# Quarter transfers, a wider first composition stage and a new instruction order in a gated-aggregation and triple-convolution kernel

## The chip, the cores and the metric

The kernel runs on one core of a Trainium2 chip. The metric is device microseconds of one execution. Engines are named as the profile names them: PE is TensorE (PEld its weight loads), DVE is VectorE, ACT is ScalarE, POOL is GpSimd, SP is SyncE, which here issues every DMA.

## The reference, cut to what matters

The input x is 8 images of 32 channels by 64 x 64, float32. `_gn` with 32 groups over 32 channels is a normalisation of each channel of each image.

```python
def _forward(x, gate_w, gate_b, value_w, geom_w, geom_b, pw_w, pw_b):
    gate = einsum('bchw,rc->brhw', x, gate_w) + gate_b
    mu = softmax(gate, axis=1)
    v = einsum('bchw,dc->bdhw', x, value_w)
    patches = the 3x3 neighbours of v, zero padded
    g = einsum('bchw,gc->bghw', x, geom_w) + geom_b
    theta, raw_base, raw_hyp = g.reshape(Bb, 3, R, L)
    sig_u, sig_s = base * exp(hyper), base * exp(-hyper)
    kern = exp(-(pu / sig_u) ** 2 - (ps / sig_s) ** 2)
    w = mu * kern
    w = w / (sum(w, axis=(1, 2)) + 1e-06)
    agg = einsum('brsl,bcsl->brcl', w, patches)
    return einsum('bkhw,ok->bohw', agg, pw_w) + pw_b

x = x + _forward(_gn(x), ...)
x = x + conv3x3(conv3x3(conv3x3(_gn(x), w1), w2), w3)
```

Per pixel and each of R = 4 mixtures, nine tap weights are made from the pixel's own channels. The three convolutions in a row have nothing between them.

## The kernel before, in words

An image lies on 128 partitions as four quarters of 16 rows by 32 channels. Since the kernel of the taps is the same for opposite neighbours, nine taps become five: the pixel itself and four sums of opposite pairs.

For image i the steps are these. `load_x(i)` brings x into one of three buffers (`xraw`). `gn1_stats`, `gn1_sums` (two PE products that add up the quarters), `gn1_spread`, `gn1_scale`, `gn1_rstd` (POOL) and `gn1_bias` make the first norm's scale and shift. ACT applies them twice: `norm1` into `xc`, `norm1_padded` into `xn`, whose edge rows the two DMAs of `halo` fill; `pair_sum` (POOL) makes the pair sums `xs`. `geometry` is 8 PE products (16 records) into `geo_ps`. `tap_weights` is a chain of 29 small DVE operations with 7 ACT parts between them. `values` transposes one of ten units (five taps, two halves of the image) into one of two banks, and `mult` on DVE multiplies it with its tap weights, 2048 columns at a time (L1060). Each half needs four sums of products: per image and half the table `SUMS` says whether DVE (V, L1070), POOL (G, L1877) or PE (T, inside `transpose_sums`) makes each; images 1 to 7 have one G in each half, fourteen in all. `sums_out` (ACT) evicts, `pointwise` (PE) and `residual` (DVE) end the first block. `gn2_...` is the second norm (L887 is the third operation of `spread` in both norms, sixteen times in all), `norm2` writes `y`, and `by_slots` copies it by 16 DMAs of 32 partitions into `xq`, the layout in which the convolutions read it.

The three convolutions are composed into one of 7 x 7, with corrections for the edges. `turn` and `take_turn` turn the weights round; `first_weights` (PE, L380) composes w2 with w3 into `v_sb`, evicted by `take_first` (ACT); `second_weights` (PE, L403) composes that with w1, evicted by `take_second` (ACT) into `kb` and `kt`. Per image `convs` then makes 60 terms: for each half of the columns 14 main ones of 512 columns (L433), and small ones for rows, columns and corners at the edges. `conv_term` splits each into two products of 64 output channels that run side by side. `result` (ACT) evicts and `store` writes the image out.

Float32 products appear as two records each, transposes as one. Every engine's program is a straight list written out by hand (in the order that a search found), and engines wait for each other by semaphores; each engine, and SP's queue, runs its list strictly in order. So an instruction that waits holds everything behind it on its engine.

The change touches `load_x` (L254, with the weights' and constants' DMAs at L258 to L264 inside it, after image 0's load), `store` (L291), `first_weights` (L380), `take_first` (L1625), the waits that count their semaphores, and the five lists. In the list of before, PE began so:

```python
            fold(0, 0)
            turn(0)
            fold(0, 1)
            turn(1)
            gn1_sums(0, 0)
            first_weights(0)
            gn1_sums(0, 1)
            first_weights(1)
            geometry(0)
            first_weights(2)
            gn1_sums(1, 0)
            first_weights(3)
```

Of the kernel before, what the change touches and what calls it, by code (L numbers as in the profile page):

```python
# [12 lines left out]
G = 4  # L13
QR = H // G
# [38 lines left out]


PAIRS = (((0, 2),), ((0, 0),), ((0, 1), (1, 0)), ((0, 2), (1, 1), (2, 0)), ((1, 2), (2, 1)), ((2, 2),), ((2, 0),))
FIRST_SEGS = {0: ((0, 3, 1), (2, 1, 6)), 1: ((0, 3, 2),), 2: ((0, 3, 3), (0, 1, 0))}
# [19 lines left out]
def conv_l0_l1_kernel(nc, x, geo_w, geo_bias, val_w, pw_t, pw_b, w1, w2, w3, ident, sel_quarter,  # L76
                      masks, consts, out):
    ctx = ExitStack()
    with ctx:
# [6 lines left out]
        def sem(name):  # L86
# [50 lines left out]
            "p (e f) -> p e f", e=STEPS)  # L137
        outb = sb("outb", [P, 2, H // 4, W])
# [106 lines left out]
        def _(sp):  # L245
# [4 lines left out]
            def load_x(j):  # L250
                if j >= N_X:
                    wait(x2_done, 2 * (j - N_X) + 2)
                src = x[j, :, :, :].rearrange("c (g r) w -> g c (r w)", g=G)
                sp.dma_start(xraw[:, j % N_X, :], src).then_inc(x_in[j % N_X], 16)  # L254
                if j == 0:
                    for dst, src in ((sel1_sb, sel_quarter), (val_w_sb, val_w), (geo_w_sb, geo_w),
                                     (geo_bias_sb, geo_bias)):
                        sp.dma_start(dst[:, :], src).then_inc(front_consts_in, 16)  # L258
                    for dst, src in ((consts_sb, consts), (ident_sb, ident), (pw_t_sb, pw_t), (pw_b_sb, pw_b)):
# [49 lines left out]
            by_slots(1, 3)  # L309
            store(0)  # L310
            halo(4)
# [12 lines left out]
            store(2)  # L324
            load_x(7)
            halo(6)
# [22 lines left out]
            for n in range(2):  # L349
                wait(out_st[n], 16 * (IMAGES // 2))  # L350

        @block.tensor
        def _(pe):
# [16 lines left out]
            def first_weights(n):  # L370

                if n == 0:
                    pe.wait_ge(turned, 2)
                if n >= N_CONV:
                    pe.wait_ge(v_out, n + 1 - N_CONV)
                rows = range(2 * n, min(2 * n + 2, STEPS))
                terms = [(e, a, b, seg) for e in rows for a in PAIRS[e] for b in range(3) for seg in FIRST_SEGS[b]]
                for k, (e, (a, a2), b2, (b, m, at)) in enumerate(terms):
                    to = (e - 2 * n) * STEPS * C + at * C
                    mm = nc.tensor.matmul(conv_ps[n % N_CONV][:, to:to + m * C], w2_sb[:, 2 * b2 + a2 if a2 < 2 else 6 + b2, :],  # L380
                                          w3_sb[:, b:b + m, 2 - a, :], start=k == 0,
                                          stop=k == len(terms) - 1, skip_group_check=True)
                mm.then_inc(first_pe, 1)

            def second_weights(n, part):

                if n == 0 and part == 0:
                    pe.wait_ge(v_out, 4)
# [3 lines left out]
                for seg in range(max(len(SEGS[b]) for b in range(3)) * 3):  # L392
                    for half, i in enumerate(ROWS2[n]):
                        if part >= len(FROM[i]) or seg % 3 >= len(SEGS[seg // 3]):
# [9 lines left out]
                                              v_sb[rows, e, at * C:(at + m) * C], start=part == seg == 0, stop=last,  # L404
# [150 lines left out]

            fold(0, 0)
            turn(0)
            fold(0, 1)
            turn(1)
            gn1_sums(0, 0)  # L560
            first_weights(0)
            gn1_sums(0, 1)
            first_weights(1)
            geometry(0)
            first_weights(2)
            gn1_sums(1, 0)
            first_weights(3)
            values(0, 0)
            values(0, 1)
            second_weights(0, 0)  # L570
            gn1_sums(1, 1)
            second_weights(1, 0)
            second_weights(1, 1)
            geometry(1)
            second_weights(2, 0)
            second_weights(2, 1)
            gn1_sums(2, 0)
            second_weights(2, 2)
            values(0, 2)
            gn1_sums(2, 1)  # L580
            values(0, 3)
            second_weights(3, 0)
            second_weights(3, 1)
            second_weights(3, 2)
            values(0, 4)
            values(0, 5)
            second_weights(4, 0)
# [3 lines left out]
            values(0, 7)  # L591
            transpose_sums(0, 2)
            values(0, 8)
            transpose_sums(0, 3)
            values(0, 9)
            second_weights(4, 1)
            pointwise(0, 0)
            geometry(2)
            values(1, 0)
            second_weights(5, 0)  # L600
            values(1, 1)
# [3 lines left out]
            transpose_sums(0, 7)  # L605
            values(1, 2)
            second_weights(6, 0)
            pointwise(0, 1)
            values(1, 3)
            values(1, 4)  # L610
            values(1, 5)
            gn2_sums(0, 0)
            gn1_sums(3, 0)
            gn2_sums(0, 1)
            values(1, 6)
            transpose_sums(1, 0)
            transpose_sums(1, 1)
            values(1, 7)
# [1416 lines left out]
```

## Time and profile before

| what | us |
|---|---|
| three runs, in order | 532.97, 548.08, 546.44 |
| median | 546.44 |
| the profiled execution's own time | 540.62 |
| its span, first to last instruction | 538.7 |
| PE busy | 477.7 (89%) |
| DVE busy | 370.1 (69%) |
| ACT busy, POOL busy | 150.2, 145.2 |
| mean granted clock of TensorE | 0.94 |

The span is 1.9 us shorter than the execution's own time; what lies around it is start and end. Busy time is no measure of how well PE is used, only of when it has something to do. The idle time of an engine matters where the engine is the one that others wait for.

### The profile page before, as it was taken

Reading aid. Unit: us, or ns where it says so; the run is one execution under the profiler, and the core shown is the slowest. Engines: PE = TensorE matmul, PEld = TensorE weight load, DVE = VectorE, ACT = ScalarE, POOL = GpSimd, SP = SyncE. Lnnn points to the kernel's source line nnn. Section 1 sums busy time; section 2 is a strip of 40 time slices with the busy share of each in tenths; the row PEclk is TensorE's granted clock in tenths of the full one; section 3 lists DMA queues with packets and bytes.
Section 4 is the critical chain, followed back from the end, with each engine's and each line's share of the span. In section 5 each row is a group of like instructions: output and inputs, shape, how many; then the busy total and the mean of one; then the engine's idle time right before and its main releaser. Section 6 shows DMA issues by size and latency. Waiting matters only on the chain. (4 is left out here: it accounts for less than half of the span.)

```text
span 538.7 us, 8815 instructions
## 1 busy us (share of the span) xinstructions
PE 477.7 (89%) x3692; PEld 299.3 (56%) x3692; DVE 370.1 (69%) x499; ACT 150.2 (28%) x247; POOL 145.2 (27%) x75
## 2 busy tenths in 40 slices
PE   0898999954698979999999997999799999999991
PEld 0898899844454544564546453465357545554451
DVE  2213499996987996999599936998978669930000
ACT  0512726512340134121712072025211440111000
POOL 0150003331903370345035400382316103300000
PEclk9999669995999997999999998999969999999997
DMA  5200000000301031003112111201003103103201
GB/s 103 86 5 0 6 1 2 5 23 18 85 6 40 0 88 39 16 29 88 41 42 65 32 43 58 61 17 24 4 1 86 41 1 86 39 1 83 44 1 39
DMA packets 26967, 19.51 MB, mean 36 GB/s; under 512 B 21104, under 2 KB 21680, under 8 KB 26928
## 3 DMA queue, kind: packets, MB, share of 16 engines
q1 hardware_dynamic: 26928, 18.95, 14.6%
q8 instruction: 29, 0.48, 0.4%
q14 instruction: 10, 0.08, 0.0%
HBM read 5.16 MB, written 4.19 MB: 17 GB/s over the span
## 5 line engine op out<-in xcount | busy, mean ns | idle before, releaser
L433 PE MATMUL conv_ps<-xq,kb 128*64 128x512 f32 x768 | 190.1, 627 | 4.1 <-DMA xq<-y 2.4
L1060 DVE TENSOR_TENSOR prod<-val_ps,tapw 128x2048 f32<-128x2048 f32 x80 | 181.0, 2280 | 8.3 <-PE val_ps L486 7.3
L433 PEld LDWEIGHTS conv_ps<-xq,kb 128*64 128x64 f32 x768 | 56.5, 139 | 86.1 <-issue 85.7
L1877 POOL TENSOR_TENSOR prod<-prod 128x2048 f32<-128x2048 f32 x14 | 64.0, 4569 | 92.8 <-DVE prod L1060 92.8
L1903 POOL TENSOR_TENSOR xs<-xn 128x1024 f32<-128x1024 f32 x32 | 68.6, 2158 | 69.5 <-PE val_ps L486 66.9
L503 PEld LDWEIGHTS agg_ps<-ident_sb,prod 128*128 128x128 f32 x688 | 76.4, 143 | 15.9 <-issue 11.7
L503 PE MATMUL agg_ps<-ident_sb,prod 128*128 128x128 f32 x688 | 83.0, 276 | 0.8 <-DVE prod L1070 0.8
L1653 ACT ACTIVATE agg<-agg_ps 128x512 f32<-128x512 f32 x64 | 37.9, 596 | 90.7 <-PE agg_ps L503 90.4
L1070 DVE TENSOR_TENSOR prod<-prod 128x2048 f32<-128x2048 f32 x23 | 54.3, 2359 | 0.0
L486 PE MATMUL val_ps<-ident_sb,xs 128*128 128x128 f32 x256 | 43.8, 298 | 6.2 <-DVE prod L1060 6.2
L486 PEld LDWEIGHTS val_ps<-ident_sb,xs 128*128 128x128 f32 x256 | 30.5, 152 | 27.1 <-issue 13.5
L1670 ACT ACTIVATE outb<-conv_ps,gn 128x512 f32<-128x512 f32 x16 | 11.0, 686 | 97.3 <-PE conv_ps L447 97.3
L1863 POOL TENSOR_TENSOR gn<-gn 128x1 f32<-128x1 f32 x8 | 6.6, 823 | 102.7 <-DVE gn L892 102.7
L433 PE MATMUL conv_ps<-xq,wmid 128*64 128x512 f32 x128 | 32.2, 610 | 0.0
L403 PE MATMUL conv_ps<-xq,w_sb 64*128 64x160 f32 (+2 forms) x154 | 24.6, 374 | 1.9 <-ACT kb L1647 1.9
L1867 POOL TENSOR_TENSOR gn<-gn,powers 128x2 f32<-128x2 f32 x8 | 6.0, 747 | 75.0 <-DVE gn L892 75.0
L380 PE MATMUL conv_ps<-outb,w_sb 64*128 64x96 f32 (+1 forms) x110 | 24.3, 410 | 0.0
L380 PEld LDWEIGHTS conv_ps<-outb,w_sb 64*128 64x128 f32 x110 | 23.7, 328 | 0.2
L403 PE MATMUL conv_ps<-xq,w1n_sb 64*128 64x32 f32 (+2 forms) x168 | 22.9, 334 | 0.6 <-ACT kt L1647 0.6
L468 PEld LDWEIGHTS geo_ps<-geo_w_sb,xc 128*128 128x128 f32 x128 | 19.2, 238 | 6.4 <-issue 4.1
L436 PEld LDWEIGHTS conv_ps<-xq,kt 128*64 128x64 f32 x448 | 16.4, 137 | 10.6 <-issue 10.6
L403 PEld LDWEIGHTS conv_ps<-xq,w1n_sb 64*128 64x128 f32 x168 | 21.0, 256 | 1.4 <-ACT kt L1647 0.9
(116 smaller groups left out, 445.4 us busy)
## 6 DMA issues: line engine op xcount, KB each, us to landing
xq<-y SPq DMA_DIRECT2D x128, 70.0 KB, 2.1
xraw<-in_x SPq DMA_DIRECT2D x8, 512.0 KB
out_y<-outb SPq DMA_DIRECT2D x8, 512.0 KB
xn<-xn SPq DMA_DIRECT2D x16, 24.8 KB, 1.8
outb<-in_w SPq DMA_DIRECT2D x1, 384.0 KB, 5.6
outb<-in_w SPq DMA_DIRECT2D x1, 192.0 KB, 8.4
outb<-in_w SPq DMA_DIRECT2D x1, 96.0 KB, 5.7
sel_sb<-in_sel_quarter SPq DMA_DIRECT2D x1, 64.0 KB, 3.4
```

Of the source, the lines that this page charges most:

```text
L380: mm = nc.tensor.matmul(conv_ps[n % N_CONV][:, to:to + m * C], w2_sb[:, 2 * b2 + a2 if a2 < 2 else 6 + b2, :], w3_sb[:, b:b + m, 2 - a, :] ...
L403: mm = nc.tensor.matmul(conv_ps[half][:, to * C:(to + m) * C], w[rows, 4 * b + half + a, :], v_sb[rows, e, at * C:(at + m) * C], start=par ...
L433: mm = nc.tensor.matmul(bank[part, :], w, src[:, every, cols], start=n == 0, stop=False)
L436: mm = nc.tensor.matmul(bank[part, q * W // 2:(q + 1) * W // 2], kt[:, half, LEFT + m, :], src[:, line, cols], start=False, stop=False)
L468: mm = nc.tensor.matmul(geo_ps[:, k * GEO:(k + 1) * GEO], xc[:, i % 2, k * P:(k + 1) * P], geo_w_sb[:, :], start=k == 0, stop=k == K8 - 1, ...
L486: mm = nc.tensor.matmul(val_ps[u % 2][:, kk * P:(kk + 1) * P], src, ident_sb[:, :], is_transpose=True, start=kk == 0, stop=kk == KK - 1, s ...
L503: mm = nc.tensor.matmul(agg_ps[n % N_AGG][:, kk * P:(kk + 1) * P], product(i, TAPS * h + b)[:, at0:at0 + P], ident_sb[:, :], is_transpose= ...
L1060: v.tensor_tensor(dst, val.unsqueeze(2).to_broadcast([P, B, R, C]), wgt.unsqueeze(3).to_broadcast([P, B, R, C]), ALU.mult).then_inc(mult_d ...
L1070: v.tensor_tensor(product(i, TAPS * h + a), product(i, TAPS * h + a), product(i, TAPS * h + b), ALU.add).then_inc(add_v, 1)
L1653: s.activation(agg[:, n % G, :], agg_ps[n % N_AGG][:, :], ACT.Copy).then_inc(agg_sb, 1)
L1877: p.tensor_tensor(product(i, TAPS * h + a), product(i, TAPS * h + a), product(i, TAPS * h + b), ALU.add).then_inc(add_g, 1)
L1903: p.tensor_tensor(xs[:, n], xn[:, a[0], a[1]], xn[:, b[0], b[1]], ALU.add).then_inc(pairs_done, 1)
```

## The change

Every load of an image, and every store, becomes four DMAs of 32 partitions, and what waits for them counts 64 in place of 16. The constants and weights have a function of their own: eight constants go behind image 0's load, the three weight tensors behind image 1's. `first_weights` makes 34 products in place of 55, with more columns in each, in eight pieces (three parts each of pieces 0 and 1, one each of 2 and 3) that the list can place singly; pieces 0 and 1 make half of the 32 output channels each, for the inner 5 x 5 steps, 2 and 3 the edges and corners. The rows of `v_sb` lie the other way round, and `take_first` has five evictions in place of four. The lists of all five engines are in a new order; `SUMS` and the number of product buffers are as before, and no sum goes by DMA, as in the kernel before.

```diff
-                src = x[j, :, :, :].rearrange("c (g r) w -> g c (r w)", g=G)
-                sp.dma_start(xraw[:, j % N_X, :], src).then_inc(x_in[j % N_X], 16)
+                for g in range(G):
+                    sp.dma_start(xraw[C * g:C * g + C, j % N_X, :],
+                                 x[j, :, QR * g:QR * g + QR, :].rearrange("c r w -> c (r w)")).then_inc(x_in[j % N_X], 16)
+
+            def load_weights(n):
+                if n == 0:
+                    for dst, src in ((sel1_sb, sel_quarter), (geo_w_sb, geo_w), (geo_bias_sb, geo_bias),
+                                     (val_w_sb, val_w)):
                         sp.dma_start(dst[:, :], src).then_inc(front_consts_in, 16)
+                elif n == 1:
+                    for dst, src in ((ident_sb, ident), (consts_sb, consts), (pw_t_sb, pw_t), (pw_b_sb, pw_b)):
                         sp.dma_start(dst[:, :], src).then_inc(back_consts_in, 16)
+                else:
...
-                dst = out[j, :, :, :].rearrange("c (q s) w -> s c q w", s=4)
-                sp.dma_start(dst, outb[:, j % 2, :, :]).then_inc(out_st[j % 2], 16)
+                for s in range(4):
+                    dst = out[j, :, :, :].rearrange("c (q s) w -> c q s w", s=4)[:, :, s, :]
+                    sp.dma_start(dst, outb[C * s:C * s + C, j % 2, :, :]).then_inc(out_st[j % 2], 16)
 
             load_x(0)
+            load_weights(0)
+            load_weights(1)
             load_x(1)
+            load_weights(2)
             load_x(2)
...
+            def first_weights(n, part):
+
+                bank = conv_ps[n % N_CONV]
+                if part == 0:
+                    if n < N_CONV:
+                        pe.wait_ge(turned, 2)
+                    else:
+                        pe.wait_ge(v_out, n + 1 - N_CONV)
+                if n < 2:
+                    to = bank[:, 0:25 * C // 2].rearrange("p (e f o) -> p e f o", e=5, f=5)
+                    src = w3_sb[:, :, 0:3, n * C // 2:(n + 1) * C // 2].rearrange("p b r o -> p r b o")
+                    terms = [(part, b, to[:, 2 - part:5 - part, b:b + 3, :], src) for b in range(3)]
+                elif n == 2:
+                    edge = bank[:, 0:10 * C].rearrange("p (e f) -> p e f", e=2)
+                    corner = bank[:, 10 * C:14 * C].rearrange("p (e f o) -> p e f o", e=2, f=2)
+                    terms = [(0, b, edge[:, 0, b * C:(b + 3) * C], w3_sb[:, :, 0, :]) for b in range(3)]
+                    terms += [(2, b, edge[:, 1, b * C:(b + 3) * C], w3_sb[:, :, 2, :]) for b in range(3)]
+                    terms += [(2 * e, 2 - 2 * f, corner[:, e, f], w3_sb[:, 2 * f, 2 * e, :])
+                              for e in range(2) for f in range(2)]
+                else:
+                    edge = bank[:, 0:10 * C].rearrange("p (f e) -> p f e", f=2)
+                    terms = [(a, 2 - 2 * f, edge[:, f, (2 - a) * C:(5 - a) * C],
+                              w3_sb[:, 2 * f, 0:3, :].rearrange("p r o -> p (r o)")) for f in range(2) for a in range(3)]
+                end = n >= 2 or part == 2
+                for k, (a2, b2, to, src) in enumerate(terms):
+                    mm = nc.tensor.matmul(to, w2_sb[:, 2 * b2 + a2 if a2 < 2 else 6 + b2, :], src,
+                                          start=part == k == 0, stop=end and k == len(terms) - 1, skip_group_check=True)
+                if end:
+                    mm.then_inc(first_pe, 1)
...
+            gn1_sums(0, 0)
+            gn1_sums(0, 1)
             fold(0, 0)
+            fold(0, 1)
+            geometry(0)
             turn(0)
-            fold(0, 1)
             turn(1)
...
             gn1_sums(1, 0)
             values(0, 0)
             values(0, 1)
+            gn1_sums(1, 1)
+            first_weights(0, 0)
+            first_weights(0, 1)
+            first_weights(0, 2)
+            first_weights(1, 0)
+            first_weights(1, 1)
+            first_weights(1, 2)
+            first_weights(2, 0)
+            geometry(1)
+            first_weights(3, 0)
             second_weights(0, 0)
...
             fold(0, 0)
+            norm1(0)
+            norm1_padded(0)
+            fold(0, 1)
+            tap_weights(0, 0)
             take_turn(0)
+            tap_weights(0, 1)
             take_turn(1)
             take_first(0)
-            fold(0, 1)
-            norm1_padded(0)
-            norm1(0)
+            tap_weights(0, 2)
+            norm1(1)
             take_first(1)
+            norm1_padded(1)
+            tap_weights(0, 3)
+            tap_weights(0, 4)
             take_first(2)
             take_first(3)
+            tap_weights(0, 5)
+            tap_weights(0, 6)
             take_second(0, 0)
             take_second(0, 1)
```

The second list in this diff is ACT's. On DVE, `gn1_stats(0)` goes ahead of `centre_table(0)`, which waits for the constants, and from image 0 to image 7 the operations of neighbouring steps are interleaved otherwise. Ahead of `gn2_bias(0)` DVE has, from the first mult on, all ten mults of image 0 and five of image 1. `convs(0, 0, 1)`, the first convolution term, stands on PE behind `values(1, 9)`; before it stood behind `values(2, 1)`.

## Rows read from the trace of the kernel before

**Rows 1.** Busy time by stage (us: span, PE, PEld, DVE, ACT, POOL; clock; DMA).

```profile
48.60:112.00 63.40, 59.68 (x541) 56.35 (x540) 50.49 (x79) 33.09 (x58) 10.59 (x6) 0.84 0.01 3
112.00:145.70 33.70, 15.64 (x111) 12.28 (x111) 28.84 (x37) 8.80 (x15) 16.88 (x7) 0.80 0.20 50
145.70:465.00 319.30, 306.28 (x2370) 167.46 (x2371) 268.56 (x333) 90.64 (x148) 107.30 (x44) 0.96 0.16 40
465.00:528.40 63.40, 62.47 (x524) 31.13 (x523) 11.03 (x16) 6.39 (x9) 1.05 (x2) 1.00 0.13 29
```

**Rows 2.** What PE waited for (total us, times, longest), whole span.

```profile
PE pw_ps L459 <- DMA pw_b_sb<-in_pw_b: 14.3, 1, 14.3
PE geo_ps L530 <- DVE mv L880: 10.1, 2, 8.0
...
PE geo_ps L530 <- DVE geo L946: 3.8, 1, 3.8
PE pw_ps L545 <- DVE gn L887: 3.4, 1, 3.4
```

**Rows 3.** Timeline (start, us): SP's issues, and DVE's first reads of two loads.

```profile
115.52 0.60 SPq L254 DMA_DIRECT2D xraw<-in_x  x1
...
125.31 1.29 DVE L878 BATCH_NORM_STATS2 st<-xraw 128x6 f32<-128x512 f32 x2 [4.00 <-DMA xraw<-in_x]
...
133.86 10.05 SPq L285 DMA_DIRECT2D xq<-y  x16
...
320.17 0.59 SPq L254 DMA_DIRECT2D xraw<-in_x  x1
...
327.80 1.29 DVE L878 BATCH_NORM_STATS2 st<-xraw 128x6 f32<-128x512 f32 x2 [4.51 <-DMA xraw<-in_x]
```

**Rows 4.** DMA issues: KB each, median us from issue to landing.

```profile
xq<-y SPq DMA_DIRECT2D x128, 70.0 KB, 2.1
...
pw_t_sb<-in_pw_t SPq DMA_DIRECT2D x1, 16.0 KB, 2.8
pw_b_sb<-in_pw_b SPq DMA_DIRECT2D x1, 0.5 KB, 9.4
```

**Rows 5.** Busy time in three short stretches (columns as in rows 1).

```profile
14.00:24.00 10.00, 9.04 (x41) 8.09 (x41) 2.35 (x9) 4.88 (x7) 0.55 (x1) 1.00 0.26 99
...
332.00:340.00 8.00, 6.82 (x26) 2.60 (x26) 8.00 (x7) 1.99 (x4) 2.40 (x1) 0.79 0.39 92
388.00:400.00 12.00, 10.29 (x40) 6.47 (x42) 8.46 (x6) 0.00 (x0) 2.35 (x2) 0.57 0.00 1
```

**Rows 6.** Timeline of SP: the issue of the last store.

```profile
528.44 0.60 SPq L291 DMA_DIRECT2D out_y<-outb  x1
```

**Rows 7.** Timeline, from the head to the first convolution: PE, DVE, ACT.

```profile
18.12 4.47 PE L380 MATMUL conv_ps<-outb,w_sb 64*128 64x96 f32 x20
...
23.03 10.87 PE L380 MATMUL conv_ps<-outb,w_sb 64*128 64x96 f32 x50
33.83 3.67 PE L468 MATMUL geo_ps<-geo_w_sb,xc 128*128 128x64 f32 x16
...
67.32 2.28 DVE L1060 TENSOR_TENSOR prod<-val_ps,tapw 128x2048 f32<-128x2048 f32 x1
...
132.47 1.26 ACT L1663 ACTIVATE y<-x,gn 128x1024 f32<-128x1024 f32 x1 [1.99 <-DVE gn L896]
...
145.69 1.54 PE L433 MATMUL conv_ps<-xq,kb 128*64 128x512 f32 x6 [1.69 <-issue]
```

**Rows 8.** The page's group of the first composition stage (busy us, mean ns).

```profile
L380 PE MATMUL conv_ps<-outb,w_sb 64*128 64x96 f32 (+1 forms) x110 | 24.3, 410 | 0.0
```

**Rows 9.** Timeline of POOL and DVE at 385 us.

```profile
385.12 4.51 POOL L1877 TENSOR_TENSOR prod<-prod 128x2048 f32<-128x2048 f32 x1 [9.38 <-DVE prod L1060]
385.21 4.45 DVE L887 SCALAR_TENSOR_TENSOR gn<-gn,mv 128x1 f32<-128x1 f32 x1
```

**Rows 10.** Line 887 alone: duration ns, min/median/max.

```profile
L887 DVE SCALAR_TENSOR_TENSOR gn<-gn,mv x16: 219/219/4445, 18.5 to 483.8; 128x1 f32<-128x1 f32 x16
```

More of the change, by code:

```diff
@@ L349, in _ @@
             for n in range(2):
[L350 removed]
+                wait(out_st[n], 64 * (IMAGES // 2))
         @block.tensor
@@ L403, in second_weights @@
                         mm = nc.tensor.matmul(conv_ps[half][:, to * C:(to + m) * C], w[rows, 4 * b + half + a, :],
-                                              v_sb[rows, e, at * C:(at + m) * C], start=part == seg == 0, stop=last,
+                                              v_sb[rows, STEPS - 1 - e, at * C:(at + m) * C], start=part == seg == 0, stop=last,
                                               skip_group_check=True)
@@ L591, in _ @@
             values(0, 7)
+            second_weights(3, 0)
             transpose_sums(0, 2)
+            transpose_sums(0, 3)
             values(0, 8)
-            transpose_sums(0, 3)
+            geometry(2)
+            pointwise(0, 0)
             values(0, 9)
-            second_weights(4, 1)
-            pointwise(0, 0)
-            geometry(2)
             values(1, 0)
-            second_weights(5, 0)
-            values(1, 1)
+            second_weights(3, 1)
             transpose_sums(0, 4)
@@ L689, in _ @@
+            values(3, 9)
+            convs(1, 43, 46)
+            geometry(5)
+            convs(1, 46, 56)
+            values(4, 0)
             transpose_sums(3, 0)
+            convs(1, 56, 60)
+            convs(2, 0, 1)
+            values(4, 1)
             transpose_sums(3, 1)
-            values(3, 7)
+            convs(2, 1, 2)
             transpose_sums(3, 2)
             transpose_sums(3, 3)
-            values(3, 8)
-            convs(1, 36, 37)
-            gn1_sums(5, 0)
+            convs(2, 2, 3)
@@ L1115, in _ @@
             gn1_scale(0)
+            centre_table(0)
             gn1_bias(0)
@@ L1203, in _ @@
             tap_weights(2, 5)
+            tap_weights(2, 6)
+            tap_weights(2, 7)
+            tap_weights(2, 8)
             mult(1, 1)
-            tap_weights(2, 6)
+            tap_weights(2, 9)
             mult(1, 2)
@@ L1482, in _ @@
             tap_weights(7, 3)
+            tap_weights(7, 4)
+            tap_weights(7, 5)
+            residual(5, 1)
+            tap_weights(7, 6)
+            gn2_stats(5, 1)
+            tap_weights(7, 7)
+            tap_weights(7, 8)
+            tap_weights(7, 9)
+            gn2_spread(5)
+            tap_weights(7, 10)
+            tap_weights(7, 11)
+            mult(6, 1)
+            gn2_scale(5)
+            tap_weights(7, 12)
+            mult(6, 2)
+            gn2_bias(5)
+            mult(6, 3)
+            tap_weights(7, 13)
+            add_products(6, 0, 1)
+            mult(6, 4)
+            mult(6, 5)
             mult(6, 6)
@@ L1724, in _ @@
             sums_out(0, 7)
-            take_second(6, 0)
+            take_second(3, 0)
             tap_weights(2, 2)
+            take_second(3, 1)
+            take_second(4, 0)
+            take_second(4, 1)
             tap_weights(2, 3)
+            tap_weights(2, 4)
+            take_second(5, 0)
             norm2(0)
-            tap_weights(2, 4)
+            tap_weights(2, 5)
             sums_out(1, 0)
+            take_second(5, 1)
             sums_out(1, 1)
```

805 lines of the change are left out of this document (376 added, 429 removed).

## Prediction

> **What bounds the kernel now.** I read the stages first [rows 1], then what TensorE waited for [rows 2], then the loads and stores behind the longest waits [rows 3 to 6], then the head [rows 7, 8]. The profiled span is 538.7 us, and TensorE is busy for 306.3 of the 319.3 us between 145.7 and 465, and for 62.5 of the 63.4 after them: in these stages it is the bound. It loses time in three places. At the start it waits 14.3 us for constants [rows 2]. Between 112 and 145.7 it works only 15.6 of 33.7 us, because the first image's chain on VectorE is late [rows 1]. At the end nothing but the last store runs: it is issued at 528.44, and the span ends 10.3 us after that [rows 6]. VectorE is second: 268.6 of 319.3 us, so 50.7 us of slack there.
>
> The loads of x are slow. That of image 3 is issued at 115.52, and VectorE, idle for 4.0 us, first reads it at 125.31: 9.8 us. That of image 7 takes from 320.17 to 327.80, 7.6 us, with VectorE idle for 4.5 [rows 3]. While nothing but x is being loaded (14 to 24 us), the DMA share is 0.26 at 99 GB/s, as if four of sixteen engines moved everything [rows 5].
>
> **The change: loads and stores.** Each 512 KB transfer becomes four of 32 partitions. The nearest row for such pieces is that of the slot copies: 16 of 70 KB, each 32 partitions wide, are issued within 10.05 us, 0.63 each [rows 3], and the page's issue list gives 2.1 us from issue to landing [rows 4]. Four pieces then cost 4 x 0.63 = 2.5 us of issue and, as the last one lands, 2.1 to 2.8 us more (2.8 is pw_t's) [rows 4]: some 5 us against 7.6 to 9.8. Lower end: 4 us, when issue alone counts; upper end: as now. I take 5. It adds 48 issues on SP's queue, 30 us over the span; what stands behind a load or store in that queue comes three issues (1.9 us) later: the slot copies above all, for which the convolutions wait. I cost that at nothing, as SP waits between them (a load at 115.52, the next copies at 133.86 [rows 3]); without that cover it is 1.9 us each time.
>
> The Trainium skill, DMA: Bandwidth & Descriptors, section "Why a DMA increments its semaphore by 16 and not by 1", says that the engines are counted from the outermost dimension of both patterns: 4 here before, 16 after. By that rule the share of 0.26 is no accident, and the trace agrees.
> The same page, section "Bandwidth", speaks against the change: it wants transfers gathered to a megabyte, and its fit has about 2 us fixed for each. If those fell one after another, four pieces would take about 9 us, an estimate from that page, and nothing would be won. The slot copies in a row every 0.63 us, each 2.1 us long, speak against that; it is a rival below.
>
> *End.* 10.3 us after the last issue become 2.5 of issue and 2.8 of landing, about 5.3: -5 us (bounds -6 and 0).
>
> *Start.* Before, the last constant that PE waits for landed 9.4 us after its issue, when the one issued just ahead of it needed 2.8 [rows 4]: I read it as their share on the four engines that still carried x. After: x's pieces end their issue at 0.73 + 4 x 0.6 = 3.1, eight constants at 0.47 follow to 6.9, and with 2.8 for landing the first four are there at 7.8, all at 9.7 (upper end: 14.3 as now).
>
> **The change: the order of the head.** Before, the first norm's second sum stood behind twenty products of the first composition stage (4.47 us), and geometry(0) behind fifty more (10.87 us), so geometry(0) ran at 33.83 for 3.67 us and VectorE started at 37.5 [rows 7]. After, PE does both sums, the folds and geometry(0) before anything else. From the first constants, 7.8: the norm's steps took 6.5 us with 4.0 of it in the queue, so 2.9 with centre_table between, 10.7; ScalarE, after fold, has normed at 12.0 (1.25 us); geometry 3.7: VectorE starts at 15.8, not 37.5.
>
> From there to the first mult took 29.8 us (to 67.32 [rows 7]). Now ScalarE's queue has take_first(0) ahead of tap_weights(0, 2), and take_first(2), (3) ahead of tap_weights(0, 5). Whatever waits behind them waits for the first composition, so that is on the path. Its cost: 110 records (two to a product; 66 of 96 columns and 44 of 32, a mean of 70) took 24.3 us [rows 8], 0.22 each. The 34 products are 68 records of 144 (36), 96 (24) and 32 columns (8). Six records of 512 columns, two side by side, take 1.54 us [rows 7], 0.51 a pair, so 1 ns a column, which leaves 0.15 us fixed: 36 x 0.294 + 24 x 0.246 + 8 x 0.182 = 17.9, against 24.3: -6.4 us. If runs of 16 numbers read slower than long runs, the saving falls to nothing (upper end, 24); if the fixed part is shared, 14 (lower end). The head is priced by the head's own rows throughout, slower as they are than later ones.
>
> PE after 15.8: turns, sums and two values to 20.3, first_weights(0) and (1) to 30.7, (2) to 35.3, geometry(1) to 38.9, (3) to 41.8, its eviction to 42.3. Then ScalarE's Square 0.6, VectorE 2.3, Exp 0.6, VectorE 3.4 and tap_weights(1, 0) 0.7: the first mult begins at 50, not 67.3: -17.3 us.
>
> **From the first mult to the first convolution.** Before: 65.2 us to the second norm at 132.47, then 13.2 for the norm and the 16 slot copies, to 145.69 [rows 7, 3]. In the new order VectorE has 15 mults of 2.28, three sums of 2.3, and small operations for 22 us ahead of gn2_bias(0): 63 us, and with waits as before but the load's 4.0 us some 68. So 50 + 68 + 13 = 131, against 145.7: -14.7. PE allows it: of its 75.3 busy us between 48.6 and 145.7 [rows 1] 74 remain, from second_weights(0) at 42, so 116 without idle time. Ends: 117 (-28) and 145.7 (0).
>
> **The long stage.** PE's work does not change here: 306.3 + 62.5 us. What can go is 13.0 + 0.9 us of idle time and the half-speed stretches. Two waits, of 2.1 us (10.1 less 8.0) and 3.8, end with a norm's sum or geometry behind a late load [rows 2]; after the second the clock is 0.79 for 8 us [rows 5], which costs 6.82 x 0.21 = 1.4, and I count as much for the first. With loads in 5 us these go: -8.7. Over the whole stage the clock is 0.96 [rows 1]: 306.3 x 0.04 = 12.3 us lost at the lower of its two levels, 1.2 and 2.4 GHz, of which 2.8 are counted. The other 9.5, and the other waits, 8.0, hang on the order; 7.8 of these 17.5 are one event, a wait of 3.4 us behind a VectorE instruction and 10.29 x 0.43 = 4.4 at 0.57 of the clock after it [rows 2, 5]. A new order may meet all of the 17.5 us again (0) or none (-17.5). I take a quarter away, -4.3, since that event looks like a coincidence. Sum for the stage: -13.
>
> **Sum.** Against the profiled execution's own time: -14.7 -13 -5 = -33, 538.7 to 506, and with the 1.9 us around the span (540.62 in all) 508 us. That execution lies 1% under the median of the three runs, 546.44, and between their ends.
>
> **The rivals.**
> *The long stage packs completely.* Against: every stage of before shows some wait. For: VectorE's 50.7 us of slack. From 131: 368.8 busy less the 12.3 of half clock, 0.7 of eviction, 5.3 of store and 1.9 around the span: 495; with the convolution at 124, 488. Time: 492.
> *The head's lead is lost before the convolutions*, since take_second stands in ScalarE's queue among the tap weights and PE's second stage waits for it. For: between 48.6 and 112 PE idles 3.7 us in that very stage [rows 1]. Then convolution 0 begins at 145.7 again: 508 + 14.7 = 523.
> *The pieces are no faster than the whole*, so the transfers' fixed time falls in a row: back come 8.7, 5 and 4.6 at the start: 526. This is also the case in which that part of the change does not do what it says.
> *Slower.* GpSimd's sums of 4.5 us hold up VectorE. At 385.21 an instruction of 0.22 us took 4.45, just as long as GpSimd's sum of 385.12 ran, and PE stood 3.4 us behind it [rows 2, 9]. Each such meeting in a norm's chain cost 3.4 + 4.4 = 7.8 us. There are 14 such sums, 16 such instructions, all newly ordered. From four more meetings on the gain is used up; at five the time is 508 + 39 = 547, and at six 555. Against: the median of the sixteen is 0.219 us [rows 10], one alone is long.
> The Trainium skill, SBUF — State Buffer, section "Who interferes with whom", has that as an exclusive lock: a two-input VectorE instruction blocks for the whole of a GpSimd instruction that reads the same memory. The row agrees.
>
> **How the numbers follow.** Forecast 508: 0.52 (its own range 498 to 520). Packed, 492: 0.18. Lead lost, 523: 0.15. Pieces no faster, 526: 0.06. Slower, 555: 0.03. The rest, 0.06, is lead lost and pieces slow together, some 538. The range is 488 to 527: it leaves out the slow ends (some 0.1) and little below. Over 2% faster (about what can be told from no change) means under 530 beside 540.6: 0.52 + 0.18 + 0.15 + 0.06 less 0.02 for runs near the edge: 0.89; within 2%: 0.08; slower: 0.03.
>
> **What would show it.** Geometry(0) near 12, the first mult near 50, the first convolution near 131; no VectorE wait for x; the last store's pieces landed some 5 us after the first issue; 68 records in the first composition, some 18 us. Wrong would be: a DMA share still near 0.3 in loads, the convolution not before 140, or new waits over 15 us in the long stage.

## The result, and the profile after

Four executions of the changed kernel took 507.69, 507.4, 509.83 and 507.81 us: a median of 507.75 against 541.43 for four of the kernel before (532.97 to 548.08, so they spread much more). The ratio is 0.950, 95% interval 0.944 to 0.957; it leaves out 548.08 and 546.44, two executions of the kernel before in a slower state, while the medians differ by 6.2%. So the change makes the kernel faster by 5 to 6%. The profiled execution took 507.69 us, its span is 505.6.

Lines have moved: L455 is the main convolution (L433 before), L402 the first composition, L1091 the mult, L918 the operation of the spread that was L887, L1921 POOL's sums.

Busy time by stage of the kernel after (columns as in [rows 1]). The stages are cut where the same work is left: 124.7, near the end of values (2,1), answers to 145.7 (there values (2,1) ended at 144.0, and PE then stood idle); 437, near the end of the last values, to 465; 500.4, the end of the last eviction, to 528.4.

```profile
39.20:87.00 47.80, 43.32 (x419) 40.41 (x420) 45.87 (x70) 21.93 (x41) 9.07 (x5) 1.00 0.01 2
87.00:124.70 37.70, 28.60 (x218) 23.63 (x217) 34.89 (x44) 16.58 (x27) 18.74 (x8) 0.83 0.18 45
124.70:437.00 312.30, 304.96 (x2373) 164.82 (x2372) 269.68 (x327) 87.90 (x144) 108.31 (x42) 0.98 0.18 40
437.00:500.40 63.40, 61.48 (x520) 30.86 (x516) 10.31 (x14) 6.35 (x9) 0.70 (x1) 1.00 0.16 32
```

Set beside [rows 1] this says where the 33.1 us of span went: 21.0 before the cut at 124.7 (145.7 - 124.7), 7.0 in the long stage (319.3 - 312.3), nothing in the next (63.4 in both), 5.1 after the last eviction (10.3 - 5.2). The cuts are good to about 1 us.

The timeline of the kernel after, rows that answer to [rows 6, 7] (PE, DVE, ACT and SP's queue):

```profile
0.73 1.79 SPq L252 DMA_DIRECT2D xraw<-in_x  x4
...
5.12 1.29 DVE L909 BATCH_NORM_STATS2 st<-xraw 128x6 f32<-128x512 f32 x2 [0.32 <-DMA xraw<-in_x]
...
10.99 3.67 PE L490 MATMUL geo_ps<-geo_w_sb,xc 128*128 128x64 f32 x16 [1.17 <-ACT xc L1594]
...
19.20 13.11 PE L402 MATMUL conv_ps<-outb,w_sb 64*128 64x144 f32 x56
...
35.85 2.87 PE L402 MATMUL conv_ps<-outb,w_sb 64*128 64x96 f32 x12
...
39.74 0.69 DVE L1024 TENSOR_TENSOR expo<-trig,ch 128x512 f32<-128x512 f32 x1 [5.68 <-ACT trig L1648]
...
46.31 2.28 DVE L1091 TENSOR_TENSOR prod<-val_ps,tapw 128x2048 f32<-128x2048 f32 x1
48.51 0.22 DVE L980 TENSOR_SCALAR ch<-geo 128x128 f32<-128x128 f32 x1
...
103.85 1.26 ACT L1707 ACTIVATE y<-x,gn 128x1024 f32<-128x1024 f32 x1
...
114.74 3.53 DVE L1030 TENSOR_TENSOR expo<-expo,trig 128x256 f32<-128x256 f32 x1
...
118.39 1.36 PE L455 MATMUL conv_ps<-xq,kb 128*64 128x512 f32 x4 [1.93 <-issue]
...
128.19 6.80 PE L455 MATMUL conv_ps<-xq,kb 128*64 128x512 f32 x20
...
500.52 2.61 SPq L295 DMA_DIRECT2D out_y<-outb  x4
```

Geometry(0) runs at 10.99 in place of 33.83, the first mult at 46.31 in place of 67.32, the second norm at 103.85 in place of 132.47. The lead is 28.6 us at the norm but 21.0 at equal work: the first convolution term stands alone at 118.39, and PE comes to the rest only at 128.19, behind two values and geometry(3); for the buffers of the values it waits 1.9 and 1.1 us for VectorE's mults. These mults stand behind L1030, a two-tensor operation that takes 0.42 us at the median and took 3.53 at 114.74, beside a sum of POOL's that ran from 113.46 to 117.98.

The waits of the kernel after, and its DMA issue list (columns as in [rows 2] and [rows 4]):

```profile
PE geo_ps L552 <- DVE mv L911: 7.9, 2, 6.8
PE pw_ps L567 <- DVE gn L918: 7.0, 3, 3.3
...
DVE st L909 <- DMA xraw<-in_x: 1.8, 2, 1.5
```
```profile
xraw<-in_x SPq DMA_DIRECT2D x32, 128.0 KB, 2.8
out_y<-outb SPq DMA_DIRECT2D x32, 128.0 KB, 2.7
```

PE's 14.3 us for constants are gone; it now starts at 6.8, with the norm's first sum, as soon as VectorE's statistics are there. The waits for late loads are all but gone too. What has grown is the wait behind VectorE's norm operation, from 3.4 us to 7.0. Its two long cases, in the timeline and in the durations of that line alone:

```profile
191.46 4.50 POOL L1921 TENSOR_TENSOR prod<-prod 128x2048 f32<-128x2048 f32 x1 [19.85 <-DVE prod L1091]
191.54 4.43 DVE L918 SCALAR_TENSOR_TENSOR gn<-gn,mv 128x1 f32<-128x1 f32 x1
...
196.03 0.38 PE L567 MATMUL pw_ps<-gn,sel_sb 128*128 128x1 f32 x2 [3.16 <-DVE gn L918]
...
407.82 4.43 DVE L918 SCALAR_TENSOR_TENSOR gn<-gn,mv 128x1 f32<-128x1 f32 x1
...
412.30 0.38 PE L567 MATMUL pw_ps<-gn,sel_sb 128*128 128x1 f32 x2 [3.28 <-DVE gn L918]
```
```profile
L918 DVE SCALAR_TENSOR_TENSOR gn<-gn,mv x16: 219/219/4433, 7.7 to 455.0; 128x1 f32<-128x1 f32 x16
```

This is the event of [rows 9, 10], met once before and twice now in the long stage. The two PE waits, 6.4 us, are nearly all of the 7.3 us that PE idles in the long stage.

### The profile page after: what moved, and what is told of

The parts are those of the page before. It is cut to its first block, busy times and chain, and to the rows that moved or that the text cites. A ratio compares the mean times of both kernels' runs of the same rounds, so it can differ in the third digit from the quotient of the medians.

```text
span 505.6 us, 8780 instructions
## 1 busy us (share of the span) xinstructions
PE 468.1 (93%) x3650; PEld 287.6 (57%) x3650; DVE 377.2 (75%) x499; ACT 150.6 (30%) x248; POOL 147.1 (29%) x75
## 3 DMA queue, kind: packets, MB, share of 16 engines
q1 hardware_dynamic: 27888, 18.95, 16.8%
## 4 chain that ended last, share of the span: by engine, by line
PE 66%; DVE 20%; issue 7%; SPq 2%; ACT 1%; POOL 1%; DMA 1%; POOLq 0%; DVEq 0%
PE conv_ps L455 34%; PE agg_ps L525 11%; DVE prod L1091 9%; PE val_ps L508 6%; PE geo_ps L490 4%; PE conv_ps L402 3%; DVE gn L918 2%; PE conv_ps L458 2%; SPq L288 2%; DVE prod L1101 2%; PE pw_ps L540 2%; PE conv_ps L465 2%; POOL prod L1921 1%; DVE expo L1030 1%; PE conv_ps L469 1%
## 5 line engine op out<-in xcount | busy, mean ns | idle before, releaser
L1091 DVE TENSOR_TENSOR prod<-val_ps,tapw 128x2048 f32<-128x2048 f32 x80 | 181.5, 2284 | 24.0 <-PE val_ps L508 18.9
L455 PE MATMUL conv_ps<-xq,kb 128*64 128x512 f32 x768 | 188.9, 623 | 3.2 <-issue 1.9
L455 PEld LDWEIGHTS conv_ps<-xq,kb 128*64 128x64 f32 x768 | 54.8, 139 | 87.8 <-issue 87.4
L1947 POOL TENSOR_TENSOR xs<-xn 128x1024 f32<-128x1024 f32 x32 | 71.1, 2231 | 97.1 <-PE val_ps L508 92.3
L1921 POOL TENSOR_TENSOR prod<-prod 128x2048 f32<-128x2048 f32 x14 | 63.8, 4560 | 121.0 <-DVE prod L1091 121.0
L525 PE MATMUL agg_ps<-ident_sb,prod 128*128 128x128 f32 x688 | 85.4, 279 | 2.9 <-DVE prod L1091 2.6
L455 PE MATMUL conv_ps<-xq,wmid 128*64 128x512 f32 x128 | 32.3, 611 | 0.0
L425 PE MATMUL conv_ps<-xq,w_sb 64*128 64x160 f32 (+2 forms) x154 | 22.6, 344 | 2.7 <-ACT kb L1691 2.2
L490 PE MATMUL geo_ps<-geo_w_sb,xc 128*128 128x64 f32 x128 | 20.8, 331 | 1.5 <-ACT xc L1594 1.5
L425 PE MATMUL conv_ps<-xq,w1n_sb 64*128 64x32 f32 (+2 forms) x168 | 21.2, 312 | 0.7 <-ACT kt L1691 0.7
L1109 DVE SCALAR_TENSOR_TENSOR x<-pw_ps,pw_b_sb,xraw 128x512 f32<-128x512 f32 x16 | 11.9, 745 | 11.7 <-PE pw_ps L540 11.7
L1707 ACT ACTIVATE y<-x,gn 128x1024 f32<-128x1024 f32 x8 | 10.1, 1257 | 31.9 <-DVE gn L927 31.9
L425 PEld LDWEIGHTS conv_ps<-xq,w1n_sb 64*128 64x128 f32 x168 | 18.7, 229 | 1.2 <-ACT kt L1691 1.0
```

What stands on the lines that cost most here:

```text
L425: mm = nc.tensor.matmul(conv_ps[half][:, to * C:(to + m) * C], w[rows, 4 * b + half + a, :], v_sb[rows, STEPS - 1 - e, at * C:(at + m) * C ...
L455: mm = nc.tensor.matmul(bank[part, :], w, src[:, every, cols], start=n == 0, stop=False)
L490: mm = nc.tensor.matmul(geo_ps[:, k * GEO:(k + 1) * GEO], xc[:, i % 2, k * P:(k + 1) * P], geo_w_sb[:, :], start=k == 0, stop=k == K8 - 1, ...
L525: mm = nc.tensor.matmul(agg_ps[n % N_AGG][:, kk * P:(kk + 1) * P], product(i, TAPS * h + b)[:, at0:at0 + P], ident_sb[:, :], is_transpose= ...
L1091: v.tensor_tensor(dst, val.unsqueeze(2).to_broadcast([P, B, R, C]), wgt.unsqueeze(3).to_broadcast([P, B, R, C]), ALU.mult).then_inc(mult_d ...
L1921: p.tensor_tensor(product(i, TAPS * h + a), product(i, TAPS * h + a), product(i, TAPS * h + b), ALU.add).then_inc(add_g, 1)
```

## The experiments

Theory: each part of the change pays about what the prediction gave it (loads 8.7 in the stage and 4.6 at the start, stores 5, the 34 products 6.4), and the new order would have paid more but for the two meetings with POOL. The main rival: the order alone carries the gain. Each time is the median of four executions or more (of three for a_first55). The kernel before, measured beside them, gave medians of 543.35, 541.5, 538.47 and 541.6 us, so a difference of under 5 us between kernels that were not measured side by side can't be read. The kernel after was not measured again beside the runs below.

**One part undone: loads whole (a_load1).**

```diff
-                for g in range(G):
-                    sp.dma_start(xraw[C * g:C * g + C, j % N_X, :],
...
+                src = x[j, :, :, :].rearrange("c (g r) w -> g c (r w)", g=G)
+                sp.dma_start(xraw[:, j % N_X, :], src).then_inc(x_in[j % N_X], 16)
```

> The kernel after, with each load of x as one transfer again (four pieces undone), all else as after (507.7 us). My theory, that a whole load is carried by four of sixteen engines: image 0's x lands near 11 us, not 5, the constants behind it near 14, geometry(0) begins near 16, not 10.99, and the loads of images 3, 6 and 7, first read 4 to 6.5 us after their issue now, are waited for by 2 to 4 us each: 514 to 523 us. Rival, pieces no faster than the whole, the order alone made room: 507 to 509 us, and VectorE's waits for x as after (1.8 us in all).

Measured: 520.97 us (519.99 to 522.51), +13.2. Waits and timeline of this kernel:

```profile
DVE st L908 <- DMA xraw<-in_x: 20.5, 7, 7.6
...
PE geo_ps L551 <- DVE mv L910: 17.3, 3, 14.1
```
```profile
12.40 1.29 DVE L908 BATCH_NORM_STATS2 st<-xraw 128x6 f32<-128x512 f32 x2 [7.61 <-DMA xraw<-in_x]
```

VectorE reads image 0 at 12.40; in the kernel after it did so at 5.12. That is 7.3 of the 13.2 us at the head; most of the rest lies in the long stage, with six later waits for x. The pieces pay.

**One part undone: stores whole (a_store1).** The four DMAs of `store` become the one of before.

> The kernel after, with each store as one transfer again. Theory: only the last store is on the path; its 5.1 us after the first issue become 10.3: 513 us. Rival, that the seven stores before it also hold up loads and slot copies on the shared queue: 516 or more, with waits of VectorE or PE for x or xq. Rival, nothing gained: 508.

Measured: 512.15 us (505.61 to 516.34), +4.4, with a span of 510.1 whose last store is issued at 499.87: 10.2 us to the end, as in [rows 6]. The spread is wide; the profile says the same.

**One part undone: the first stage in 55 products (a_first55).** `first_weights` and `take_first` of before, in the new order; parts 1 and 2 do nothing.

> The kernel after with the first composition stage of before (55 products in four blocks, placed where the pieces' first parts stand). Theory: take_first stands ahead of the tap weights in ScalarE's queue, so the 8 us more of this stage (24.3 against 16.0) come onto the path of the first mult: from 46.3 to about 54, and the whole to 513 to 516 us. Rival, the lead of the head is absorbed before the convolutions (VectorE waits for TensorE there anyway): 507 to 510 us.

Measured: three executions at 513.03 to 514.16, median 513.45, +5.7, at the edge of what can be read. The fourth, the profiled one, took 665.63 us and is left out, so this kernel has no profile to read.

**One part alone in the kernel before: loads in four (b_load4).**

> The kernel before, with the loads of x alone in four pieces. Theory (undoing this in the kernel after cost 13 us): x and the constants behind it land early, so PE starts near 9.5 and not 14.3, and VectorE's three waits for x (11.3 us in all) go: 528 to 533 us beside 543. Rival, that the old order absorbs the lead, since geometry(0) stands behind the first composition anyway: 536 to 541 us.

Measured: 524.68 us (522.44 to 531.64), 16.8 under the 541.5 beside it; ratio 0.968 [0.962, 0.973]. In its waits and its timeline:

```profile
DVE st L879 <- DMA xraw<-in_x: 1.0, 1, 1.0
```
```profile
8.05 0.45 PE L460 MATMUL pw_ps<-ident_sb,x 128*128 128x128 f32 x1 [8.05 <-DMA pw_b_sb<-in_pw_b]
```

More than expected. PE started at 8.05, not at 14.34: the constants issued behind x land earlier too, which the prediction had put down to engines shared with x [rows 4].

**One part alone in the kernel before: the head's order (b_headorder).** The lists of PE, DVE and ACT up to the second composition stage as in the kernel after; all else as before (the start of PE's list, then of ACT's):

```diff
+            gn1_sums(0, 0)
+            gn1_sums(0, 1)
             fold(0, 0)
+            fold(0, 1)
+            geometry(0)
             turn(0)
-            fold(0, 1)
             turn(1)
...
             fold(0, 0)
+            norm1(0)
+            norm1_padded(0)
+            fold(0, 1)
+            tap_weights(0, 0)
             take_turn(0)
...
```

> The kernel before, with the head's order of the kernel after alone (norm sums and geometry(0) first on PE, the statistics ahead of the constants' table on VectorE, ScalarE's head list), transfers and the 55 products as before. Theory: geometry(0) begins near 18 and not 33.8, but the 24 us of the first composition now stand in ScalarE's queue ahead of the tap weights: first mult near 60, not 67.3; 534 to 538 us. Rival, the lead is lost before the convolutions: 541 to 545. Rival, the head's order is the whole gain of the order: below 530.

Measured: 544.07 us, ten executions; ratio 1.008 [1.003, 1.013]. The rival holds: nothing is won. Its waits:

```profile
PE geo_ps L530 <- DVE mv L880: 24.5, 3, 14.0
...
DVE st L878 <- DMA xraw<-in_x: 23.3, 5, 7.5
```

Geometry(0) does come at 18.20 and the first mult at 60.88, 6.4 us earlier than in [rows 7]. But an engine that is earlier only meets the whole loads earlier: VectorE now waits 23.3 us for x, 11.3 in the kernel before. The quarter loads pay without the head's order, the head's order doesn't pay without them.

**All but the order (b_allbutorder).** The kernel before with loads and stores in four and the 34 products.

> The kernel before with four-piece loads and stores and the 34 products, in its own order (pieces placed where the four blocks stood). Theory, parts that add: 543 - 13 - 5 - 6 = 519, which leaves some 11 us to the new order. Rival, the parts pay only in the new order: 528 or more. Rival, the order is worth nothing by itself: 506 to 510.

Measured: 515.19 us, ratio 0.950 [0.945, 0.955]. That is 26.3 us under the 541.5 beside it without any of the new order, so the main rival falls. For the order 515.19 - 507.75 = 7.4 us are left, give or take the 5 us above. The whole new order with the transfers and products of before was not run.

**The lock taken out of the kernel after (a_onein).** The spread's operation made d x d + var, with d a difference of means, from two tensors of 128 x 1; written as below it has one tensor and two operands of one number per partition, and computes the same:

```diff
-                v.scalar_tensor_tensor(t[:, 2:3], t[:, 1:2], t[:, 1:2], mv[:, 1:2],
-                                       ALU.mult, ALU.add).then_inc(sem_v, 1)
+                v.tensor_scalar(t[:, 2:3], t[:, 1:2], t[:, 1:2], mv[:, 1:2],
+                                ALU.mult, ALU.add).then_inc(sem_v, 1)
```

> The kernel after with the third operation of the norms' spread made from one tensor input and two per-partition scalars (tensor_scalar) in place of a two-tensor scalar_tensor_tensor; the computation is the same. Theory: at 191.5 and 407.8 this instruction took 4.43 us, not 0.22, because GpSimd's sum held the port of its second input, and PE waited 3.2 and 3.3 us behind it, with a lower clock after: both stalls go, 498 to 502 us. Rival, the instruction is blocked whatever its inputs, or the next two-input instruction takes the stall over: 506 to 509 us.

Measured: 496.23 us (495.23 to 497.06), 11.5 under the kernel after; ratio to before 0.912 [0.907, 0.917]. The same meeting in its timeline, the line alone, and its long stage:

```profile
191.18 4.56 POOL L1921 TENSOR_TENSOR prod<-prod 128x2048 f32<-128x2048 f32 x1 [19.85 <-DVE prod L1091]
...
191.27 0.27 DVE L918 TENSOR_SCALAR gn<-gn,mv 128x1 f32<-128x1 f32 x1
```
```profile
L918 DVE TENSOR_SCALAR gn<-gn,mv x16: 272/273/276, 7.5 to 444.7; 128x1 f32<-128x1 f32 x16
```
```profile
124.62:426.31 301.69, 300.80 (x2370) 163.50 (x2371) 261.07 (x326) 87.75 (x144) 108.06 (x42) 0.99 0.19 41
```

POOL's sum runs as before and VectorE passes beside it. From the end of values (2,1) to the end of the last values, PE now idles 0.9 of 301.7 us, at a clock of 0.99; the same work took 311.6 us in the kernel after (124.95 to 436.59). So each of the two meetings had cost 5.0 us there. The Trainium skill, SBUF — State Buffer, section "Who interferes with whom", puts the lock down to a second input from SBUF; by that rule an instruction with at most one such input passes, as long as it is in none of the modes that use both of VectorE's ports. The rows of L918 agree, if an operand of one number per partition isn't counted as an input.

One tensor input alone isn't enough. L998 is also a `tensor_scalar`, on 128 x 128; it takes 0.22 us at the median, but beside POOL's sum of 242.93 it was held as long as that ran:

```profile
244.44 3.13 DVE L998 TENSOR_SCALAR ch<-ch 128x128 f32<-128x128 f32 x1
```

The exception that the Trainium skill makes for the modes with both ports would cover it, but no run here shows the mode. This stall, that of L1030 and eight more of VectorE's beside POOL (of 0.6 us or more) are left in this kernel. In the long stage they cost PE next to nothing, since VectorE has slack there; Behind L1030's, ahead of most of the first convolutions, PE still waits 2.9 and 1.5 us for VectorE; no run here takes it out.

**The same in the old order (b_onein, b_allbutorder_onein).**

> The kernel before, with the norms' third operation made from one tensor input. Theory: the one stall of 4.45 us at 385 goes, with PE's wait of 3.4 and the lower clock after it: 533 to 537 us beside 543. Rival, that GpSimd's sum then stalls the next two-input instruction and nothing is won: 541 to 545.

> The kernel before with loads and stores in four and the 34 products, in its own order (515.19 us), and here also with the spread of the group statistics written with one tensor input. That kernel meets the lock once (PE pw_ps <- DVE gn, 3.4 us at once, some 7.8 us with the sums and transposes behind it). Theory (each lock costs about 6 us in any order, and a one-input spread returns it): 507 to 510 us, so that the new order alone, both without locks, is worth 11 to 14 us (against 496.23). Rival (the one event of the old order was hidden): 513 to 516 us, and the order alone is worth 17 to 20.

Measured: 538.88 us (531.21 to 540.75; ratio 0.988 [0.978, 0.997]), by the medians some 2.6 saved, which four executions so far apart don't settle; and 507.61 us (504.4 to 509.55), 7.6 under the same kernel with the lock, as the theory said. In b_allbutorder the wait had been this, and it is gone in the other:

```profile
PE pw_ps L562 <- DVE gn L908: 3.4, 1, 3.4
```

The traces settle the price better than the times. The same work, from the end of values (2,1) to the end of the last values, in the kernel before and in b_onein (columns as in [rows 1]):

```profile
144.00:465.48 321.48, 306.76 (x2375) 167.80 (x2376) 270.70 (x336) 90.64 (x148) 109.35 (x45) 0.96 0.17 40
```
```profile
148.34:462.84 314.50, 301.47 (x2374) 164.87 (x2376) 265.55 (x336) 90.63 (x148) 109.49 (x45) 0.98 0.17 41
```

That is 7.0 us for the one meeting. The profiled execution of b_onein lost most of it again ahead of the stage, where no meeting is: its second norm came at 136.77, 4.3 us later than in [rows 7], and its products ran at the lower clock for longer (four records of values still take 1.12 us at 91.12, and 0.60 at 96.36). So one meeting costs 5 to 7 us of the long stage. Without locks the order is worth 507.61 - 496.23 = 11.4 us, again give or take 5. That the kernel after shows only 7.4 of it since it meets the lock once more than the old order fits these numbers, but the difference is too small to show it.

**The head pushed further (a_onein_act, a_onein_act_pe, a_onein_head).** In the kernel after, ACT's Square for the first tap weights stands behind take_first(3), and VectorE waits 5.7 us for it. First ACT's list alone:

```diff
-            take_first(0)
             tap_weights(0, 2)
             norm1(1)
-            take_first(1)
-            norm1_padded(1)
+            take_first(0)
             tap_weights(0, 3)
...
```

> The kernel after with the one-input spread (496.23 us), and ScalarE's list at the head changed: the tap weights of pixels' pieces 2 to 5 and the norm of the next group stand ahead of the evictions of the first composition stage, each eviction as late as its product allows. In the kernel after, VectorE's geometry of item 0 waits 5.7 us for the Square behind take_first(3), and the first multiplication starts at 46.3. Theory (the head is VectorE's from there to the convolutions, so an earlier start is carried through): first multiplication at 37 to 40, time 486 to 491. Rival (the values products stand on TensorE behind the second stage's composition, so VectorE waits there and the lead is lost): 494 to 497, with a longer wait of VectorE for the values' PSUM behind the first multiplications.

Measured: 495.42 us (493.46 to 504.64), the same as 496.23 within the spread. The first mult starts at 36.34 instead of 45.78, and the first convolution term 2.8 us earlier, at 114.54 instead of 117.35. Most of the rest was lost here:

```profile
50.92 0.16 DVE L915 COPY gn<-geo_ps 128x1 f32<-128x1 f32 x1 [5.29 <-PE geo_ps L552]
```

VectorE waits for two tiny products that stand in PE's list behind the first products of the second composition. Then PE's values moved forward as well, with these sums left where they were:

> As the kernel with ScalarE's changed list, and on TensorE the values products (0,2) and (0,3) moved ahead of the second stage's second product, (0,4) ahead of its third. Theory (values were what the earlier start ran into): 484 to 490, some us under the kernel with ScalarE's list alone, no long wait of VectorE for values. Rival (TensorE has no slack at the head: what is moved ahead delays the composition and so the first convolution by as much): 494 to 497.

Measured: 501.76 us (498.74 to 502.33): a loss of 5.5, which neither the theory nor the rival had. Timeline of PE and a window (columns as in [rows 1]):

```profile
45.13 0.36 PE L425 MATMUL conv_ps<-xq,w1n_sb 64*128 64x96 f32 x4
...
51.89 1.11 PE L508 MATMUL val_ps<-ident_sb,xs 128*128 128x128 f32 x4 [3.16 <-DVE prod L1091]
52.93 0.91 PE L425 MATMUL conv_ps<-xq,w_sb 64*128 64x160 f32 x4
53.62 0.58 PE L425 MATMUL conv_ps<-xq,w1n_sb 64*128 64x96 f32 x4
```
```profile
52.00:70.00 18.00, 18.00 (x125) 17.31 (x126) 9.97 (x10) 6.30 (x12) 2.40 (x2) 0.54 0.00 1
```

The moved values wait 3.2 us for a buffer, with the composition behind them in PE's queue, and after the pause the granted clock is 0.54 up to 70 us, the lower level for nearly all of that stretch: four records of the same form take 0.58 us where they took 0.36. Last, the sums moved forward too:

> The kernel with the one-input spread, ScalarE's changed list, and on TensorE the group sums of item 2 (gn1_sums(2, 0)), then values (0,2) and (0,3), right behind the second stage's first product, and values (0,4) behind its third. With ScalarE's list alone VectorE waited 5.3 us at 45.6 for these sums, which stood behind two products of the second stage, and the early start was lost there. With the values moved but the sums left (501.76 us), VectorE still waited 2.8 us for the sums, TensorE then stood 3.2 us at 48.7 for a buffer that VectorE had not yet read, and its granted clock was 0.54 from 52 to 70. Theory (the sums held the lead): VectorE doesn't stop between 36 and 52, TensorE doesn't either, first convolution of item 0 by 112, time 487 to 492. Rival (any pause of TensorE at the head is answered with a lower clock behind it, and the earlier values make one): 495 to 502, with a granted clock under 0.8 somewhere between 45 and 75.

Measured: 496.27 us over six executions (491.43 to 502.8), the rival's time. The wait had moved to the next queue:

```profile
54.23 0.42 DVE L1008 TENSOR_TENSOR ch<-ch 128x256 f32<-128x256 f32 x1 [5.47 <-ACT ch L1629]
```

ACT's part of the tap weights stands behind the evictions of the second composition. The values that were moved ahead did not make these later: the next product of the composition began at 44.69, and at 44.47 in a_onein_act, where PE had waited 2.2 us for a buffer first. It ended 1.05 us later (51.62 for 50.57), because more of it ran at the lower clock. The clock column shows 1.00 from 45 to 75, but the durations don't: in a_onein_act four records of this form take 0.36 us from 50.21 on, here 0.58 up to 57.81.

```profile
57.81 0.58 PE L425 MATMUL conv_ps<-xq,w1n_sb 64*128 64x96 f32 x4
...
59.41 0.36 PE L425 MATMUL conv_ps<-xq,w1n_sb 64*128 64x96 f32 x4
```

So the low clock that the rival named was there until some 58 us. That an earlier pause made it is not shown, and how the loss divides between ACT's queue and the clock stays open. Some nine us of earlier start are in the traces, and none of these lists carries more than some three of them to the convolutions. None of the three kernels can be told apart as faster than the one with the one-input spread alone.

## Why the prediction was right, step by step

The forecast was 508 us and the result is 507.75, but two terms were wrong by about 6 us each, in opposite directions. The parts and the mechanisms are right in the main; that the sum agrees to within a microsecond is luck. So is the start: the sum begins at one execution of the kernel before, 540.62 us, while the four lie between 532.97 and 548.08.

*Transfers: right.* Five us for a load in pieces: image 0's is issued at 0.73 and read at 5.12. No wait of VectorE's for x over 1.5 us remains. Undoing the loads cost 13.2 us, where the prediction had 8.7 and 4.6. The rival "pieces no faster" fell. The end: 5.1 for -5, and 4.4 when undone.

*The first composition: right in the main.* 68 records in 13.11 + 2.87 = 16.0 us against 17.9, so 8.3 us less than before for the predicted 6.4; undone it cost 5.7. The split into 1 ns a column and 0.15 us fixed is not the head's own: the first figure comes from the convolutions at 145.69.

*The head: -14.7 was too little.* At equal work it is -21.0. Geometry(0) at 10.99 and the first mult at 46.31 were 1 and 4 us better than forecast. The mis-sized term is "small operations for 22 us" and "with waits ... some 68" between the first mult and the norm. It took 57.5 us: 15 mults and 3 sums, 41.1, then some 16 for small operations, and 0.6 of idle time, where I had put 5. The durations of the 65 small operations do add up to 21.7, but VectorE begins an operation before the last has ended (at 48.51, where the mult of 46.31 ends at 48.59), and their sum counts these overlaps twice. From the norm to the first term it was 14.5 for 13, and that term came at 118.39, not 131; but as told above, 10 us passed before the next ones, so the lead at the term overstates the gain. "Lead lost" did not come.

*The long stage: -13 was too much.* The stage gave 7.0, and what follows it nothing. The failing step is "I take a quarter away, -4.3, since that event looks like a coincidence". The waits for loads and the other order-dependent waits went altogether, more than the quarter; but the new order met POOL's lock twice. Without it the same work takes 301.7 us in place of 311.6, and the time is 496, close to the rival "packs completely" at 492. The rival "slower" had the right mechanism, a price per meeting of 7.8 (measured 5.0 in the kernel after, 7.0 in the kernel before) and the wrong count: one more meeting, not four. Fourteen sums and sixteen norm operations stand in chains that run side by side in every image. The one meeting of before was the only count there was of how often such an order meets, and it should have been carried over as one, not written down as chance.

*What the parts add to.* Undone singly: 13.2 + 4.4 + 5.7, and 7.4 for the order, 30.7 of the 33.7 us between the medians.

## What to carry to other kernels

An order that brings an engine forward pays only if what it then meets is early too: the same head order gave nothing with whole loads and was part of a gain with quarters. Where GpSimd works beside VectorE, look for tiny two-tensor operations in a latency chain and write them with one tensor and per-partition operands; for 128 x 1 that ended the stalls, and it was worth 11.5 us here, about as much as the whole new order. Read the new durations afterwards: a one-tensor operation on 128 x 128 was still held. When a stall vanishes, follow the next queue: three rewritten heads moved the same wait from ACT to PE and back to ACT. Price an engine's work by the busy time of a window, not by adding up durations that overlap.

## What was not expected of the hardware

The clock column of the profile shows 1.00 from the start of the kernel after to 87 us. Yet in the second composition four records of 64 x 96 take 0.58 us up to 51.41 and 0.36 us from 54.62 on:

```profile
51.41 0.58 PE L425 MATMUL conv_ps<-xq,w1n_sb 64*128 64x96 f32 x4
...
54.62 0.36 PE L425 MATMUL conv_ps<-xq,w1n_sb 64*128 64x96 f32 x4
```

These are the two durations that a_onein_act_pe shows with a granted clock of 0.54 and of 1.00. The 16 records of a geometry agree: 3.67 us at 10.99 and at 32.24, 1.90 at 72.82. By these durations the first 50 us ran at the lower level, 1.2 GHz, and the column told nothing of it. When the durations change differs from trace to trace: some 52 us here, 58 in a_onein_head, over 90 in b_onein. So an estimate for the head has to use the head's own rows, and a 1.00 in the column there has to be checked against durations.
